# A gated attention block with a sign-weight FFN: the elementwise work of a step in another order

## The reference, cut to what matters

```python
xn = _layernorm(x)
q, k, v = (_causal_dwconv(_silu(xn @ W), conv_w) for each of q, k, v)   # 4 taps per channel
z, a, b = xn @ Wz, xn @ Wa, xn @ Wb
q = q * cos + rot_half(q) * sin;  q = q / norm(q)                       # k the same
out = 0
for s in range(4):                                                      # each token sees 4 tokens
    out = out + (sum_d(q * lag(k, s)) * scale * sigmoid(lag(a, s) * b)) * lag(v, s)
out = (out * rsqrt(mean(out**2) + 1e-6) * norm_w * _silu(z)) @ Wout
g = _silu(relu(xn @ sign(up).T * up_scale) @ sign(down).T * down_scale * output_scale)
return x + out * g
```

## Time and profile before

| | |
|---|---|
| median of 3 runs | 1356.13 us (1355.78 to 1356.19) |
| the profiled execution | 1355.53 us, of which the span is 1353.7 us |
| granted TensorE clock, mean | 0.998 of full speed |
| busy, share of the span | PE 97%, weight loads 82%, DVE 73%, ACT 58%, POOL 36% |
| prologue, up to about | 40 us |
| attention loop | about 40 to 921 us |
| passage into the FFN | about 921 to 945 us |
| FFN and output projection | from about 945 us |

### The profile page before, as it was taken

How to read it: one execution, slowest core, us unless ns; L and a number is a source line. 1 busy time by engine, 2 the same in 40 slices (tenths; PEclk the granted TensorE clock), 3 DMA queues, 4 the chain that set the end, 5 groups by cost and what they waited for, 6 DMA issues and landing times. The chain is left out here.

```text
span 1353.7 us, 22528 instructions
## 1 busy us (share of the span) xinstructions
PE 1318.3 (97%) x6568; PEld 1103.8 (82%) x6568; DVE 982.0 (73%) x1531; ACT 784.5 (58%) x1504; POOL 485.1 (36%) x634
## 2 busy tenths in 40 slices
PE   6999999999999999999999999999999999999998
PEld 5688888888888888888888888887888888888886
DVE  7889999999999999999999999996122223334342
ACT  5666676767766666666666676766543444422221
POOL 6245454545545455555555454553000000000001
PEclk9999999999999999999999999999999999999999
DMA  8366656666566566665666656555710101156543
GB/s 262 81 131 127 134 116 151 133 130 136 120 146 135 124 132 134 140 141 121 130 144 121 147 119 139 123 118 137 243 40 24 47 15 55 50 184 203 170 133 139
DMA packets 141562, 171.83 MB, mean 127 GB/s; under 512 B 32720, under 2 KB 69584, under 8 KB 141264
## 3 DMA queue, kind: packets, MB, share of 16 engines
q1 hardware_dynamic: 114160, 121.48, 32.0%
q0 software_dynamic: 27360, 49.82, 21.6%
HBM read 62.58 MB, written 25.30 MB: 65 GB/s over the span
## 5 line engine op out<-in xcount | busy, mean ns | idle before, releaser
L1254 DVE TENSOR_TENSOR hid_lo<-relu,hid_hi 128x512 fp32r<-128x512 f32 x64 | 44.3, 692 | 169.1 <-ACT hid_hi L1246 169.1
L798 DVE SCALAR_TENSOR_TENSOR y_k<-u_k,cw_k,y_k 128x512 f32<-128x512 f32 x192 | 146.1, 761 | 27.4 <-ACT y_k L651 20.6
L798 DVE SCALAR_TENSOR_TENSOR y_q<-u_q,cw_q,y_q 128x512 f32<-128x512 f32 x192 | 144.4, 752 | 22.5 <-ACT y_q L651 14.8
L1346 POOL TENSOR_TENSOR g_buf<-g_buf,up_raw 128x512 f32<-128x512 f32 x3 | 3.8, 1279 | 356.2 <-DVE g_buf L1406 356.2
L510 POOL TENSOR_TENSOR rnorm<-norms,neg_half 128x8 f32<-128x8 f32 x64 | 122.6, 1915 | 9.5 <-POOL norms L506 8.5
L1242 ACT ACTIVATE relu<-bank,us_sb 128x512 f32<-128x512 f32 x64 | 44.1, 690 | 123.3 <-PE bank L1265 123.3
L540 POOL DMA_DIRECT2D sq_sum<-out_sq x62 | 53.9, 869 | 162.4 <-DVE norms L831 112.4
L1366 ACT ACTIVATE hid_hi<-o_raw 128x512 fp32r<-128x512 f32 x64 | 40.2, 630 | 116.0 <-PE bank L1475 97.3
L1426 DVE TENSOR_TENSOR hid_lo<-o_raw,hid_hi 128x512 fp32r<-128x512 f32 x64 | 43.8, 690 | 79.9 <-ACT hid_hi L1366 79.9
L690 ACT ACTIVATE down_raw<-y_q 64x512 f32<-64x512 f32 x64 | 40.5, 632 | 103.3 <-PE bank L1036 103.3
L526 POOL TENSOR_TENSOR rq_win<-rq_win,const 128x32 f32<-128x32 f32 x64 | 30.1, 471 | 194.9 <-DMA rq_win<-rq_scratch 194.9
(11 more groups left out here) (193 smaller groups left out, 3711.8 us busy)
## 6 DMA issues: line engine op xcount, KB each, us to landing
swapped_q<-y_q SPq DMA_DIRECT2D x128, 128.0 KB, 2.4
swapped_k<-y_k SPq DMA_DIRECT2D x128, 128.0 KB, 2.4
o_scratch<-o_buf SPq DMA_DIRECT2D x64, 256.0 KB, 3.4
o_raw<-o_scratch SPq DMA_DIRECT2D x64, 256.0 KB, 4.0
down_raw<-down_raw POOLq DMA_DIRECT2D x63, 256.0 KB, 3.4
y_v<-down_raw POOLq DMA_DIRECT2D x63, 256.0 KB, 4.3
sq_sum<-out_sq POOLq DMA_DIRECT2D x62, 256.0 KB, 3.3
raw_q<-in_wq SPq DMA_DIRECT2D x16, 256.0 KB, 3.1
```

Of the source, the lines that this page charges most:

```text
L798: nc.vector.scalar_tensor_tensor(y[n][:, g % 2, :], u[n][:, g % 2, i:i + CH], cw[n][:, bass.ds(h * TAPS + i, 1)], y[n][:, g % 2, :], ALU.m ...
L1254: nc.vector.tensor_tensor(hid_lo[:, j % HS, :], relu[:, j % 2, :], hid_hi[:, j % HS, :].bitcast(fp32), ALU.subtract).then_inc(hid_lo_done, 1)
```

## The change

ACT's and DVE's `step` are written in another order. No operation is added or dropped. On ACT `square_out` moves ahead of k's silu, v's silu and taps move ahead of the squares of q, the squares of k go behind `save_spill`, and the split of v's weights (in the last head the two `up_signs`) goes behind those. On DVE the taps of q alternate with rope parts of the chunk before (k's part 1 and both parts 2, which so cross into the next step), the taps of k with `sum_fold` and the pair `gate_scores`, `mask_band`, the taps of v with rope's parts 0; `join_out` and `make_o` come ahead of rope's part 1 of q. Three rope parts of the last chunk stand behind the loop.

```diff
@@ ScalarE, step @@
             if not is_start(h, g):
                 silu_and_tap("q", bank_qv, h, g, c)
+            if back(h, g, 4):
+                square_out(c - 4)
+            if not is_start(h, g):
                 silu_and_tap("k", bank_kz, h, g, c)
             if g == 3 and not is_last(h):
                 split_hi("q", h + 1, c)
-            squares("q", g, c)
-            if back(h, g, 4):
-                square_out(c - 4)
             silu_and_tap("v", bank_qv, h, g, c)
             if g == 3 and not is_last(h):
                 split_hi("k", h + 1, c)
-                split_hi("v", h + 1, c)
-            elif g == 3:
-                for n in "qkvz":
-                    act.wait_ge(wlo_done[n], H)
-                ffn.up_signs(0)
-                ffn.up_signs(1)
-            squares("k", g, c)
+            squares("q", g, c)
             if at := back(h, g, 2):
                 silu_z(at[1], c - 2, bank_kz)
...
             if at := back(h, g, 3):
                 save_spill(at[1], c)
+            squares("k", g, c)
+            if g == 3 and not is_last(h):
+                split_hi("v", h + 1, c)
+            elif g == 3:
+                for n in "qkvz":
+                    act.wait_ge(wlo_done[n], H)
+                ffn.up_signs(0)
+                ffn.up_signs(1)
@@ VectorE, step @@
-            for n in "qk":
-                for i in (1, 2, 3):
-                    conv_tap(n, i, h, g, c)
+            at1, at3 = back(h, g, 1), back(h, g, 3)
+            conv_tap("q", 1, h, g, c)
+            if at1:
+                rope("k", 1, at1[1], c - 1)
+            conv_tap("q", 2, h, g, c)
+            if at1:
+                rope("q", 2, at1[1], c - 1)
+            conv_tap("q", 3, h, g, c)
+            if at1:
+                rope("k", 2, at1[1], c - 1)
+            conv_tap("k", 1, h, g, c)
+            if at1:
+                sum_fold(at1[1], c)
+            conv_tap("k", 2, h, g, c)
+            if at3:
+                gate_scores(at3[1], c - 3)
+                mask_band(at3[1], c - 3)
+            conv_tap("k", 3, h, g, c)
...
-            if at := back(h, g, 3):
-                gate_scores(at[1], c - 3)
-            if at := back(h, g, 1):
-                sum_fold(at[1], c)
-            if at := back(h, g, 3):
-                mask_band(at[1], c - 3)
+            if g == 3 and not is_last(h):
+                split_lo("q", h + 1)
+            conv_tap("v", 1, h, g, c)
             if is_start(h, g):
                 dve.wait_ge(tables_in, 32)
             rope("q", 0, g, c)
+            conv_tap("v", 2, h, g, c)
             rope("k", 0, g, c)
-            if g == 3 and not is_last(h):
-                split_lo("q", h + 1)
-            conv_tap("v", 1, h, g, c)
-            conv_tap("v", 2, h, g, c)
             if is_end(h, g):
                 conv_tap("v", 3, h, g, c)
+            if g == 3 and not is_last(h):
+                split_lo("k", h + 1)
+            if at3:
+                join_out(at3[1], c)
+                make_o(at3[0], at3[1], c - 3)
+            rope("q", 1, g, c)
+            if is_end(h, g):
                 dve.wait_ge(squares_done, NC)
                 nc.vector.tensor_tensor(fold, fold, other, ALU.add).then_inc(folded_last, 1)
             if g == 3 and not is_last(h):
-                split_lo("k", h + 1)
                 split_lo("v", h + 1)
-            for i in (1, 2):
-                rope("q", i, g, c)
-                rope("k", i, g, c)
...
-            if at := back(h, g, 3):
-                join_out(at[1], c)
-                make_o(at[0], at[1], c - 3)
...
         schedule(dve, step)
+        rope("k", 1, G - 1, NC - 1)
+        rope("q", 2, G - 1, NC - 1)
+        rope("k", 2, G - 1, NC - 1)
         sum_fold(G - 1, NC)
```

## The result

| | before | after |
|---|---|---|
| median, us (lowest to highest) | 1355.95 (1353.48 to 1356.19, 4 runs) | 1342.32 (1341.58 to 1342.71, 4 runs) |
| profiled execution, and its span, us | 1355.53, 1353.7 | 1341.58, 1339.8 |
| granted TensorE clock | 0.998 | 1.000 |
| T of step 4, us | 98.92 | 97.66 |
| T of step 63, us | 919.11 | 906.82 |

The ratio is 0.9903, with a 95% interval of 0.9886 to 0.9920: the changed kernel is 13.6 us faster, against 14.5 forecast. As before, T is the start of `turn_v` in a step. The last three rows split the 13.9 us of span: 1.3 up to step 4, 11.0 between steps 4 and 63, 1.6 behind them.

The account below looks back on a forecast made before the run. PE, busy 97%, bounds the kernel, waiting mainly for DVE's `mask_band` at head starts. Gains 12.1 (loop) + 0.8 (first steps) + 1.6 (passage) = 14.5 us off 1355.53 gave 1341.0, median 1341.6; forecast 1338.5 to 1344.5 (0.57), range 1336.5 to 1349.

Parts of the forecast that it names:

- All of the gain is PE's waiting, and most of it at head starts: Attention loop: PE loses 16.0 us behind step 4, nearly all at 15 head starts; 12.1 of it gained.
- Durations by place, and an alternation that saves 0.12 to 0.22 a tap: DVE: a tap behind the tap it reads costs 0.79 to 0.89, otherwise 0.66 to 0.67; five such taps a step.
- What the Trainium skill says: DVE: by the skill's DRAIN rule alternation would give nothing; the prediction said the trace disagrees with both halves.
- Ordinary steps at the edge, slack 0 to 0.10: Ordinary loop steps: `mask_band` ends T + 0.28 to T + 0.39, nothing lost up to T + 0.38; step stays 13.63 us.
- Heads late by 0.26, 3.9 us in all: First step of 15 heads: `sum_values` late by 0.26 to 0.45 instead of 1.12; 3.9 us lost, up to 6.8.
- First steps 0.8, between 0 and 1.7: Step 2: the 1.73 us wait for v's silu goes, most turning into a longer wait at `turn_fold`; gain 0.8.
- The passage 1.6, between 1.3 and 2.3: Passage into the FFN: z's silu comes earlier, `turn_fold` 1.95 and the last `sum_fold` 1.3 us earlier; gain 1.6.
- Slower, nothing overlaps: Rival, chance 0.10: moved taps keep 0.79, `mask_band` ends T + 0.93, about 1380 us; gain gone at T + 0.65.

Follow-up runs that it names:

- e3: The changed kernel with `gate_scores`, `sum_fold`, `mask_band` in that order behind k's first tap, ahead of its second; 1337.7 us, ratio 0.9878 against before.
- e5: The changed kernel with q's three taps side by side again and the three rope parts behind them; 1358.4 us, ratio 1.0026 against before.
- e4: The changed kernel with k's third tap between `gate_scores` and `mask_band`; 1369.6 us, ratio 1.0110 against before.
- e1: The kernel before with DVE's half of the change alone, ACT's order left old; 1347.4 us, ratio 0.9951.
- e7: The kernel before on both engines, with `sum_fold`, `gate_scores`, `mask_band` moved behind k's second tap instead of the third; 1345.6 us, ratio 0.9937.
- e10: e7 with `gate_scores`, `sum_fold`, `mask_band` in that order behind k's first tap; 1346.6 us, ratio 0.9942 against before.
- e8: e3 with q's three taps side by side; 1342.0 us, ratio 0.9909 against before.
- e9: e8 with the low-part split of the next head's k weights ahead of k's first rope product; 1341.0 us, ratio 0.9898 against before.

## Why the prediction was right

- *All of the gain is PE's waiting, and most of it at head starts:* right in the loop. It gave 11.0 of 13.9 us, and e3 shows that nothing but `mask_band`'s place held the rest of the loop's loss. The passage's 1.6 was not PE's waiting, see below.
- *Durations by place, and an alternation that saves 0.12 to 0.22 a tap:* right, and shown by e5, where the same instructions in another order cost 16 us. From q's first tap to `mask_band`'s end it took 7.24 (515.83 to 523.07) and 7.26, for 7.24 to 7.35 worked out. The pair cost 0.72 to 0.73, under the 0.75 to 0.86 that was bounded from taps. A `gate_scores` whose result the next operation reads costs 0.10 to 0.11 more than the 0.62 that it costs ahead of another.
- *What the Trainium skill says.* The section of the Trainium skill's page VectorE: DVE Perf Modes that the prediction set against the trace, The DRAIN you can't avoid, adds that a next operation that is not held starts earlier, and refers to the page's section Two Vector instructions with no wait between them. With that the rows agree (0.60 from start to start at 0.68 of length), so the prediction was too short in calling the page's rule wrong as a whole. The other sentence of the Trainium skill's section, that the semaphore costs nothing extra, stands there for eight tensor_copies. In this case a wait for the result of the operation right ahead does cost: 0.12 to 0.13 at a tap (0.79 against 0.66 to 0.67), 0.10 to 0.11 behind `gate_scores`.
- *Ordinary steps at the edge, slack 0 to 0.10:* right. `mask_band` ends at a median of T + 0.26 there and `sum_values` starts undisturbed. e5 (T + 0.45) and e4 (T + 0.72) went over that edge and paid at nearly every step.
- *Heads late by 0.26, 3.9 us in all:* the lateness was right, 0.28, by two errors against each other. The q taps came at T - 6.78 instead of T - 6.65 and `mask_band`'s end at T + 0.46 instead of T + 0.65. But from there to `sum_values` it took 0.24, as in the row of step 36 before, where I had taken the 0.05 of step 62. The reason that I gave for that choice, that a small delay is nearer to step 62, was wrong. The 0.24 belongs to the first step of the 13 heads in the hardware loop, however small the delay is; step 62 is in a head that is written out. This is the mis-sized term of the sum: 5.0 instead of 3.9, of which 1.1 to 1.5 is the longer distance to `score` behind a `sum_values` that waited, which the sum had not at all. And it fell on 13 head starts, not on 15: in step 60 `mask_band` ends at T + 0.38 and nothing is lost.
- *First steps 0.8, between 0 and 1.7:* 1.26, of which 0.13 is there at T of step 1. The mechanism was right: the transfer ahead of `turn_fold` sets the time, and it came 1.29 sooner because DVE's gate came 1.19 sooner (64.41 before, 63.22 after), not 0.6 to 1. The wait for v's silu did not turn into a longer one at `turn_fold`; 0.47 of it came back at the v projection, and `turn_fold` waits 1.50 instead of 1.80. ACT's order gave nothing here: e1 without it has the whole gain.
- *The passage 1.6, between 1.3 and 2.3:* 1.6 in the profiled executions, by luck. `turn_fold` moved by 2.21 against T of step 63 (1.95 forecast), the last `sum_fold` by 1.67 (1.3 forecast). But 1.6 is the slow stretch of the clock in before's trace, which the sum took for the order's gain: it set its 925.7 against a `turn_fold` of 927.65, which stands 4.04 behind z where e7 has 2.86, and which is 1.00 long where the earlier trace rows have 0.60. Against e7, after gains 1.0 at `turn_fold` and 0.1 at the next `score`, where PE waits 0.93 for `gate_scores`. Of the three terms this is the one whose mechanism was wrong. Without the slow stretch, 12.3 us of span were gained where 14.5 were forecast.
- *Slower, nothing overlaps:* it did not come true, the taps took 0.66 to 0.67 in their new places. But its account of how near the loss lay was too kind. It put the point at T + 0.65 in ordinary steps; e5, with T + 0.45 there and T + 0.89 at the heads, already ends at 1.0026 of before. The edge lies closer than I had it: the heads pay too, and a step that waits also pays 0.07 to 0.10 behind the wait.

What stays open: that GpSimd's gates come late in e10 is read off the timeline; no kernel moved them by themselves. And no kernel removed the z wait alone, so how far it goes with the slow stretch of the clock is not shown.

## What to carry to other kernels

When an engine is busy for 97% of the time, look for what the others hand it last, and note for each such hand-over when it is due and when it comes; here three of them (`mask_band`, and the splits of q's and of k's weights) lay within 0.5 us of their due times, and in e8 to e10 what mended one of them ran into another. Put the operation that the critical engine waits for as early as its own inputs allow, with something independent between it and what it reads: three moved operations and a split gave what a whole new order gave. Alternating dependent instructions is worth 0.1 to 0.2 us each on VectorE only as far as the shorter lap reaches one of those due times. And before a stretch of the trace is put down to the order, compare the granted clock of the two traces in that stretch: here it made 1.6 us that looked like a won wait.

## What the runs showed of the hardware that was not expected

- The time from VectorE's last instruction to the matmul that waits for it is 0.05 to 0.06 us in most steps (e4: 567.76 to 567.82) and 0.24 in the first step of each of the 13 heads in the hardware loop (after: 536.93 to 537.17; before: 543.96 + 0.70 to 544.90; 0.29 in one such step each of before, e1 and e7). It is not the start of a head as such: in steps 4 and 60 of e4 and e5, the first of heads 1 and 15, which are written out, it is 0.05 to 0.06. So the due time of `mask_band` is about T + 0.19 in those 13 steps and T + 0.38 in all others; e8, at T + 0.17, pays almost nothing there and e9, at T + 0.35, pays 0.16. In the trace the wait stands on the matmul's weight load in the one case and on a register instruction ahead of it in the other. That this is the cause was not tried.
- A group of eight matmuls that had to wait takes 0.07 to 0.10 us longer to hand over to the next group (after: 0.97 against 0.90). Over e5's loop this is 4 us more than in after's, beside 11 more of plain waiting.
- A wait can be in the trace and in no list under its name: in after it is 4.1 us at the weight loads of 13 steps, as issue, and the matmul that is 0.28 late has no idle time printed before it.
